# Two graphs' contexts ahead of two graphs' scores in TensorE's order, from the third unit on

## What is computed

```python
h = jnp.maximum(_layernorm(x, axis=-1), 0.0)
q = _heads(h @ Wq + bq)
k = _heads(h @ Wk + bk)
v = _heads(h @ Wv + bv)
scores = jnp.einsum('bhqd,bhkd->bhqk', q, k) / np.sqrt(HEAD_SIZE)
probs = jax.nn.softmax(scores + jnp.where(graph_mask, 0.0, NEG)[:, None], axis=-1)
ctx = jnp.einsum('bhqk,bhkd->bhqd', probs, v)
x = x + (merged_heads(ctx) @ Wf + bf)
```

## Time and profile before

| | |
|---|---|
| median of 3 runs | 1891.49 us (1887.21 to 1894.95) |
| the profiled execution, its own time | 1890.07 us |
| its span, first to last instruction | 1888.3 us |
| TensorE busy | 1864.7 us, 99% of the span |
| ScalarE, VectorE, GpSimd busy | 1524.4, 1474.5, 1180.1 us (81%, 78%, 62%) |
| mean granted TensorE clock | 0.994 |
| share of TensorE in the chain that ended last | 91% |
| DMA | 363.12 MB, 192 GB/s |

### The profile page before, as it was taken

One profiled execution on the slowest core, in us unless ns is written; L12 is line 12 of the kernel. 1 busy time (PEld: TensorE's weight loads), 2 busy tenths in 40 slices (PEclk: granted clock), 3 DMA queues, 4 the chain that ended last, 5 costly groups with the idle time before them and its releaser, 6 DMA issues.

```text
span 1888.3 us, 51061 instructions
## 1 busy us (share of the span) xinstructions
PE 1864.7 (99%) x15794; PEld 1081.4 (57%) x15794; DVE 1474.5 (78%) x5319; ACT 1524.4 (81%) x4553; POOL 1180.1 (62%) x1797
## 2 busy tenths in 40 slices
PE   7999999999999999999999999999999999999998
PEld 3555555555555555555555555555555555555555
DVE  7887778777777777777777777778777777777775
ACT  5888888888888888888888888888888887888885
POOL 4766666666666666666666666666666666666652
PEclk8999999999999999999999999999999999999999
DMA  6656666666666666666666666666666666666655
GB/s 189 177 172 188 203 199 195 194 189 197 204 201 184 188 196 199 202 194 186 192 199 207 198 189 193 195 196 206 197 194 184 194 204 197 192 179 186 187 170 177
DMA packets 439928, 363.12 MB, mean 192 GB/s; under 512 B 207700, under 2 KB 406888, under 8 KB 439656
## 3 DMA queue, kind: packets, MB, share of 16 engines
q1 hardware_dynamic: 439656, 359.86, 62.9%
HBM read 184.30 MB, written 175.37 MB: 190 GB/s over the span
## 4 chain that ended last, share of the span: by engine, by line
PE 91%; DVE 2%; DMA 2%; SPq 1%; ACT 1%; POOL 1%; issue 1%; POOLq 0%; DVEq 0%; ACTq 0%
PE ps_qk L646 13%; PE ps_shared L646 12%; PE ps_shared L648 12%; PE ps_shared L647 12%; PE ps_qk L647 12%; PE ps_qk L648 12%; PE ps_shared L734 9%; PE ps_scores L754 7%; DMA p_moved<-p_dram 1%; SPq L347 1%; ACT probs L945 1%; ACT x_tile L945 0%; DMA wk_raw<-in_L_gnn_Wk 0%; POOL probs L515 0%; DVE p_blocks L1185 0%
## 5 line engine op out<-in xcount | busy, mean ns | idle before, releaser
L945 ACT ACTIVATE probs<-probs,exp_bias,exp_scale 128x128 f32<-128x128 f32 x1512 | 723.3, 482 | 2.6 <-POOL exp_bias L510 2.6
L515 POOL TENSOR_TENSOR probs<-probs,row_rcp 128x768 f32<-128x768 f32 x252 | 370.2, 1469 | 536.2 <-DVE row_rcp L1209 536.2
L1219 DVE SCALAR_TENSOR_TENSOR qk_lo<-ps_qk,qk_bias,qk_hi 128x512 f16<-128x512 f32 x384 | 286.1, 749 | 125.5 <-ACT qk_hi L928 123.0
L1239 DVE CUSTOM_DVE_ANT_0 probs<-ps_scores,mask 128x128 f32<-128x128 f32 x1512 | 340.1, 287 | 1.1 <-issue 0.7
L921 ACT ACTIVATE v<-ps_shared 128x384 f32<-128x384 f32 x252 | 123.8, 491 | 252.7 <-PE ps_shared L648 252.7
L1249 DVE SCALAR_TENSOR_TENSOR x_tile<-ps_shared,out_scale,x_tile 128x384 f32<-128x384 f32 x256 | 157.9, 617 | 212.6 <-PE ps_shared L648 212.5
L928 ACT ACTIVATE qk_hi<-ps_qk,qk_bias 128x512 f16<-128x512 f32 x384 | 258.5, 673 | 38.4 <-PE ps_qk L648 38.4
L945 ACT ACTIVATION_READ_ACCUMULATOR probs<-probs,exp_bias,exp_scale 128x1 f32 x1512 | 287.8, 190 | 0.0
L504 POOL TENSOR_TENSOR x_tile<-x_tile,out_bias 128x384 f32<-128x384 f32 x256 | 258.0, 1009 | 1.1 <-DVE out_bias L1168 1.1
L522 POOL TENSOR_TENSOR ht_lo<-h_moved,ht_hi 128x384 f16<-128x384 f32 x252 | 231.1, 917 | 39.4 <-ACT ht_hi L912 38.7
L646 PE MATMUL ps_shared<-wf_hi,ct_hi 128*128 128x384 f16 x768 | 250.9, 327 | 1.7 <-DVE ct_lo L1213 1.7
(11 more groups left out here) (134 smaller groups left out, 3575.5 us busy)
## 6 DMA issues: line engine op xcount, KB each, us to landing
p_dram<-p_blocks SPq DMA_DIRECT2D x256, 384.0 KB, 2.4
p_moved<-p_dram SPq DMA_DIRECT2D x1024, 96.0 KB, 2.4
h_dram<-h_blocks SPq DMA_DIRECT2D x252, 192.0 KB, 2.2
h_moved<-h_dram SPq DMA_DIRECT2D x1008, 48.0 KB, 2.0
x_tile<-in_x SPq DMA_DIRECT2D x128, 192.0 KB, 2.9
out_x<-x_tile SPq DMA_DIRECT2D x128, 192.0 KB, 2.5
adj_u<-in_adj SPq DMA_DIRECT2D x64, 64.0 KB, 2.4
wv_raw<-in_L_gnn_Wv SPq DMA_DIRECT2D x2, 576.0 KB, 5.1
```

The source lines that it names most:

```text
L515: nc.gpsimd.tensor_tensor(probs_of(t, i), probs_of(t, i), row_rcp[i % 2][:, :].rearrange("p (a o) -> p a o", o=1) .to_broadcast([P, HEADS, ...
L945: ins = nc.scalar.activation(tile[:, s, :], tile[:, s, :], ACT.Exp, bias=exp_bias[i % 2][:, s:s + 1], scale=exp_scale[layer_of(t)][:, :], ...
L1219: nc.vector.scalar_tensor_tensor(out=qk_lo[b][:, chunk, :], in0=ps_qk[chunk % QK_BANKS][:, :], scalar=qk_bias[layer_of(t)][:, chunk // KT, ...
L1239: ins = nc.vector.tensor_tensor_reduce(tile[:, s, :], score_bank(i, s // PAIRS)[:, (s % PAIRS) * P:(s % PAIRS + 1) * P], mask[b][:, i, :], ...
```

## The change

In TensorE's `slot`, for t of 2 and more, the two contexts of an even step now stand ahead of its two scores. In slot 1 the order stays. No instruction is added or removed, and the other engines' programs are the same.

```diff
+            def contexts(t, i):
+                for pu, pi in pair_at(t, i):
+                    if exists(pu):
+                        apply_probs(pu, pi)
+
             def slot(t):
                 for i in range(PER):
                     ou, oi = graph_at(t, i, -4)
+                    if t > 1:
+                        contexts(t, i)
                     if exists(t) and i % 2 == 0:
                         score(t, i)
                         score(t, i + 1)
-                    for pu, pi in pair_at(t, i):
-                        if exists(pu):
-                            apply_probs(pu, pi)
+                    if t == 1:
+
+                        contexts(t, i)
                     if exists(t + 1):
                         for piece in PIECES[i][0] + PIECES[i][1]:
                             project_qk(t + 1, piece)
```

## The result

| | before | after |
|---|---|---|
| median | 1889.08 us of 6 runs (1885.77 to 1894.95) | 1931.28 us of 6 runs (1928.08 to 1934.17) |
| profiled execution, its span | 1890.07, 1888.3 us | 1931.20, 1929.4 us |
| TensorE busy | 1864.7 us | 1886.8 us |

The ratio is 1.0221, with a 95% interval of 1.0211 to 1.0231: 42.2 us slower. The forecast was 1935 us, by terms that add up to 44.5 us. From here on VectorE's and ScalarE's lines in the changed kernel stand 7 lines lower: `add_residual` is line 1256, `mask_and_max` 1246.

The account below looks back on a forecast made before the run. TensorE was taken as the bound, busy 1864.7 of 1888.3 us and waiting for nothing in the loop. 24.0 + 20.5 = 44.5 us on 1890.07 gives 1934.6; with the median 1.4 above that execution, forecast 1935, range 1913 to 1953.

Parts of the forecast that it names:

- Matmul boundaries: TensorE's boundaries between output projection, contexts, scores and next projections: 0.34 us before, 0.35 after, taken as 0, within 1.2 us.
- not slower: Rival: new block boundaries on TensorE save as much as the stall costs, 0.14 instead of 0.34 us; 1891.5 us, chance 0.04.
- First context: Pair's first context on TensorE: its bank is free 0.8 us before it can start, so cost 0.
- Residual: Second context waits for VectorE's add_residual on the bank of the odd step's output projection: 0.20 us at 120 places, 24.0 us.
- no cover at all: Rival: the first context hides none of the wait for the bank; 0.85 us at 120 places, 1993 us, chance 0.02.
- Late probabilities: Second context waits for SyncE's transfer p_moved, landing too late at 45 of 119 places: 20.5 us, bounds 0 and 30.
- residual only: Rival: SyncE's transfers catch up while TensorE stalls, leaving only 0.20 us per place; 1915.5 us, chance 0.14.
- Later effects: Scores end later, VectorE's mask moves about 0.2 us, ctx_lo keeps 0.65 us of room ahead of V: cost 0.
- The scores late too: Rival: VectorE's mask slips past the 0.65 us of room ahead of V, TensorE stalls again; 1953 us, chance 0.12.
- The sum: Whole kernel: 24.0 + 20.5 = 44.5 us of added time, forecast 1935 us, 2.3% slower.
- The last part: Profile after: TensorE's waits, 300 to 1700 us, rise from 1.4 to some 30 to 40 us, released by add_residual and p_moved.

Follow-up runs that it names:

- the kernel with the load behind: Changed kernel with SyncE's load of x moved behind the probabilities' transfer, store left ahead: 1917.01 us, ratio 1.0148; same edit in the kernel before: 1891.84 us, 1.0015.
- the reversed pair: Changed kernel with the two contexts in reverse order, the one waiting for the residual addition first: 2011.07 us, ratio 1.0644.
- The split: Against the kernel before, only the first context put ahead of the two scores, the second left behind them: 1907.17 us, ratio 1.0093.

## Why the prediction was right

**Matmul boundaries, 0.** Held: O to C, C to S and S to Q in the profile after are those of the earlier trace rows. The rival *not slower* needed 0.14 us for the three; they come to 0.34 again.

**First context, 0.** Held: it starts at O + 0.26 at all places, the late ones included, since what is late there is the second context. V's copy ends at O - 0.55 in the median, as before, and at O - 0.18 at the latest.

**Residual, 24.0.** Measured 23.2 by the readings of the pair; the kernel with the load behind, with some late probabilities left, stands 25.2 above its own before. The release is O + 1.11 where it stands bare. The cover of the first context is what the forecast took, and *no cover at all* is ruled out as this kernel's price (it would be the 1.0644 of the reversed pair). The rule of the Trainium skill ("Perfetto Trace Analysis", section "Optimizing Tensor Performance": independent groups of matmuls should rotate through different banks) pointed the right way, and the runs agree in sign: 0.19 us are lost per place with one group in between, 0.85 with none.

**Late probabilities, 20.5.** Measured 22.8 at 46 places, and 13.3 us of it given back by the load of x behind the probabilities. The mechanism held; that the size did is in part luck, for two errors offset each other. The first: the prediction counted a transfer as late from O + 1.06 on, which leaves 0.05 us from the landing to the start at O + 1.11. The context starts 0.14 us after the landing, as the trace of the kernel before shows at 10 late places. With that, the landings before give 25.2 us at 55 places, and not 20.5 at 45. The second: it took these landings over as they stood. After, 36 land later than O + 1.06, by 18.2 us in all, and only 24 of them are places of the forecast. With the 0.14 that is 22.0 us at 46 places. So SyncE's transfers did come a little earlier against O, as the rival *residual only* said, but by some 3 us of 25 and not all of them; that rival is out. The claim that each late landing is tied to the previous O holds for the sum and not place by place.

**Later effects, 0.** Held: the mask moved by 0.25 us, and `ct_lo` kept mostly 0.56 to 0.60 us of room ahead of V, 0.2 at the least. *The scores late too* is ruled out by TensorE's waits: between 300 and 1700 us they have none at line 754, nor for `ct_lo`.

**The sum.** 44.5 forecast, 42.2 measured between medians and 41.1 between spans, where the readings of the pairs give 43.7.

**What failed: where it would show.** The last part said that TensorE's waits should rise to some 30 to 40 us, released by the residual and by the transfer. They rose to 19.0, nearly all by the transfer. That step took a stall and a wait in the trace for the same thing. The second context starts 0.14 us late and then costs 0.05 more, and each record of a context lasts 0.27 us to its modelled end where the next starts 0.1 us after it, so the pair reads as busy for 1.72 us instead of 1.53, and 22.1 us of the loss appear as busy time. Had I judged by that view alone, I would have missed half of the cost. It stands in the weight loads' waits and in the starts.

**What failed in the experiments' expectations.** That p_moved may be moved ahead in SyncE's queue at no cost (27 and under 3 us expected, 57.4 and 50.9 measured) left out the landing of p_dram that it must wait for, and that the queue is in order. The split's 12 us left out the fresh start of two contexts instead of one (17.2 measured).

## What to carry to other kernels

When a block is moved up in an in-order engine, take every semaphore that its instructions wait for and compute when it is given, counted from the last instruction that gives it; the block may move up only as far as the latest. Two waits on one instruction don't add but nest: removing the earlier one shows the later one. And before a transfer is moved up in a queue, see what its own wait for a landing is filled with. Here the load alone moved out of that wait cost 3.7 us in the old order, store and load together 50.9.

## What the runs showed of the hardware

**DMA issues take longer while another engine's instructions are fetched.** In the kernel before, an issue that mostly takes 0.43 us takes more than 1 us 90 times from 60 us on, and 88 of these overlap a packet of the queue q8 or lie within half a microsecond of one; after, it is 87 of 88. Of all of SyncE's issues in that stretch only 14% lie so close to one, and of the 171 that overlap one, half take more than 1 us. These packets come once in some 14.6 us, 126 in all with 2.06 MB, so 16 KB each. Such an issue group in the kernel before, and the DMA queues while it lasts:

```profile
686.64 3.48 SPq L347 DMA_DIRECT2D p_moved<-p_dram  x4
```

```profile
q8 instruction: 1, 0.02, 2.6%
```

Around the issue of 1.74 us at 904.07 there is no packet of q8. TensorE has 15794 matmuls and as many weight loads in 64 units of four steps, that is some 247 instructions per pair of steps (15794 x 2 / 128), and a pair of steps takes 14.4 us, nearly the interval of the packets. So the packets drift slowly through the steps, and for some 200 us at a time they meet p_moved. The run with sixty matmuls in front moved both stretches, and there all 75 long issues lie at a packet: the packets follow TensorE's program, and the long issues follow the packets. The Trainium skill, "Runtime: NRT & Kernel Launch", section "Instruction fetch mechanics", gives 16 KiB blocks of 256 instructions, which fits the size of the packets and their interval, and calls the crossing of one mostly hidden. For TensorE it is hidden here, as far as its waits between 300 and 1700 us show, which are all for p_moved or the residual; for SyncE's issues it is not: 16.2 of the 18.7 us of waits for p_moved lie in the two stretches. By what means a fetch holds up an issue, no run here shows.

**A context costs 0.05 us more when it starts afresh** than behind another, and the boundaries between contexts, scores and projections cost the same in either order (0.34 and 0.35 us for the three). That makes it cheap to move such blocks as pairs, and dear to split them.
